# Host-side layout of weights and context in a two-layer gated cross-attention kernel, with values ahead of keys and the first layer's keys made already turned

## The reference

```
x = x + tanh(g_xattn[0]) * attn0(LN(x), ctx, ctx)   # 32 query heads, 8 key/value heads, D = 128,
                                                    # rotary q and k, masked softmax, @ Wo
x = x + tanh(g_ffn[0])   * moe(LN(x))               # 16 experts of 56, top 2, silu(gate) * up, down
x = x + tanh(g_xattn[1]) * attn1(LN(x), ctx)        # same sizes; q and k RMS-normed per head, weights given
x = x + tanh(g_ffn[1])   * lora(LN(x))              # 4 adapters of rank 16, top 2, scaled by 4
```

## Time and profile before

| | |
|---|---|
| time, median of 3 runs | 1358.91 us (1358.12 to 1359.04) |
| profiled execution: span from first to last instruction | 1356.7 us |
| PE busy | 1292.6 us (95%), 6801 matmuls |
| DVE, ACT, POOL busy | 837.7, 501.5, 496.4 us (62%, 37%, 37%) |
| mean granted PE clock | 0.982 of full |
| chain that ended last: PE, POOL, DVE, issue | 74%, 9%, 9%, 6% |
| moved by DMA | 106.97 MB |

### The profile page before, as it was taken

How to read it: one execution, slowest core, us unless ns; L and a number is a source line. 1 busy time by engine, 2 the same in 40 slices (tenths; PEclk the granted TensorE clock), 3 DMA queues, 4 the chain that set the end, 5 groups by cost and what they waited for, 6 DMA issues and landing times.

```text
span 1356.7 us, 18171 instructions
## 1 busy us (share of the span) xinstructions
PE 1292.6 (95%) x6801; PEld 1025.9 (76%) x6801; DVE 837.7 (62%) x1519; ACT 501.5 (37%) x779; POOL 496.4 (37%) x322
## 2 busy tenths in 40 slices
PE   7999999889999999999799999999999999999976
PEld 5888887567777777777688887677777777777765
DVE  4465354888878887888863234655554555555586
ACT  3343242113222222121443124654455455545522
POOL 6302302548677777785301110032332323233200
PEclk9999999889999999999899999999999999999987
DMA  7363555611222222113010004212121121211001
GB/s 263 103 185 128 183 155 179 209 47 63 78 70 70 77 70 69 47 48 109 1 55 32 1 0 118 78 40 71 40 70 70 46 87 53 70 39 39 32 1 62
DMA packets 77500, 106.97 MB, mean 79 GB/s; under 512 B 8108, under 2 KB 40884, under 8 KB 77448
## 3 DMA queue, kind: packets, MB, share of 16 engines
q1 hardware_dynamic: 76808, 104.69, 23.4%
q0 software_dynamic: 640, 1.57, 0.3%
HBM read 78.99 MB, written 27.26 MB: 78 GB/s over the span
## 4 chain that ended last, share of the span: by engine, by line
PE 74%; POOL 9%; DVE 9%; issue 6%; ACT 1%; DMA 1%; SPq 1%; POOLq 0%; DVEq 0%; ACTq 0%
PE ps_q L215 12%; PE ps_q L217 11%; PE ps_q L216 11%; PE ps_b L215 9%; PE ps_b L217 9%; PE ps_b L216 8%; PE ps_s L876 3%; PE ps_s L862 2%; PE ps_b L898 2%; POOL qT L1101 2%; POOL wo_lo L1096 2%; POOL wq_lo L690 1%; PE ps_s L257 1%; PE ps_b L458 1%; POOL p_sb L741 1%
## 5 line engine op out<-in xcount | busy, mean ns | idle before, releaser
L215 PE MATMUL ps_b<-wo_hi,o_hi 128*128 128x512 f32 x512 | 205.8, 402 | 18.2 <-POOL wo_lo L1096 12.3
L215 PE MATMUL ps_q<-hT_hi,wq_hi 128*128 128x512 f32 x512 | 211.4, 413 | 5.4 <-DVE q_t L1176 2.8
L217 PE MATMUL ps_q<-hT_hi,wq_lo 128*128 128x512 f32 x512 | 203.1, 397 | 0.0
L216 PE MATMUL ps_q<-hT_lo,wq_hi 128*128 128x512 f32 x512 | 203.1, 397 | 0.0
L217 PE MATMUL ps_b<-wo_hi,o_lo 128*128 128x512 f32 x512 | 201.4, 393 | 0.0
L216 PE MATMUL ps_b<-wo_lo,o_hi 128*128 128x512 f32 x512 | 200.9, 392 | 0.0
L215 PEld LDWEIGHTS ps_q<-hT_hi,wq_hi 128*128 128x128 f32 x512 | 96.6, 189 | 45.4 <-issue 19.0
L1251 DVE SCALAR_TENSOR_TENSOR x_sb<-ps_b,gates,x_sb 128x512 f32<-128x512 f32 x128 | 92.8, 730 | 58.4 <-PE ps_b L217 57.9
L215 PEld LDWEIGHTS ps_b<-wo_hi,o_hi 128*128 128x128 f32 x512 | 97.4, 190 | 40.8 <-issue 18.1
L1242 DVE TENSOR_TENSOR o_lo<-ps_b,o_hi 128x512 fp32r<-128x512 f32 x128 | 82.1, 683 | 65.0 <-ACT o_hi L1025 64.6
L217 PEld LDWEIGHTS ps_q<-hT_hi,wq_lo 128*128 128x128 f32 x512 | 96.5, 189 | 23.8
(11 more groups left out here) (246 smaller groups left out, 2459.1 us busy)
## 6 DMA issues: line engine op xcount, KB each, us to landing
wq_raw<-in_L_xattn_Wq SPq DMA_DIRECT2D x16, 1024.0 KB, 5.2
wo_raw<-in_L_xattn_Wo SPq DMA_DIRECT2D x16, 1024.0 KB, 5.3
kT_spill<-kT_st SPq DMA_DIRECT2D x4, 2048.0 KB, 6.9
v_hi_spill<-vs_hi SPq DMA_DIRECT2D x16, 512.0 KB, 5.5
v_lo_spill<-vs_lo SPq DMA_DIRECT2D x16, 512.0 KB, 7.2
kT<-kT_spill SPq DMA_DIRECT2D x32, 256.0 KB, 3.4
v_hi<-v_hi_spill SPq DMA_DIRECT2D x16, 512.0 KB, 3.6
v_lo<-v_lo_spill SPq DMA_DIRECT2D x16, 512.0 KB, 4.5
```

The costliest lines, as they stand in the source:

```text
L215: nc.tensor.matmul(dst, l_hi, r_hi, start=first, stop=False)
L216: nc.tensor.matmul(dst, l_hi, r_lo, start=False, stop=False)
L217: return nc.tensor.matmul(dst, l_lo, r_hi, start=False, stop=last)
```

## The change

The host passes every array in the layout in which the core wants it (`laid_out`): the context transposed, every weight transposed where it was (out, in), cut into groups and partition-major, both masks in their final layout, router and adapter weights padded to 128 columns. So PE turns no weight and no context, and each load is one transfer with long rows: the masks are one transfer instead of 16 and 4, gates one instead of two, adapters two instead of six. In particular:

- Start: the first block's work is cut by the contraction: SP loads piece k of the weights and of the context's first half in turn, ACT and DVE split them, and PE adds piece k into four banks for token tiles 0 to 3, then takes tiles 4 to 7. Position ids come through ACT's queue; ACT makes one dummy Sqrt first. One rotation table, eight indirect DMAs.
- Keys and values: the order in a column block is values 0, keys 0, values 1, keys 1, on four banks (`ps_q`, `ps_b[0:2]`); turns of layer-1 keys use `ps_b[2:4]`. Layer-0 keys are computed as (head width x tokens), weights as the stationary side, so they need no turn: DVE rotates with three operations, POOL adds straight into the staging buffer. Weight splits of the next block: ACT and POOL.
- The factor 1/sqrt(D) moves from the query table into the exponential of the first attention.
- Second attention: Wq and Wo are split like those of the first (ACT, POOL); ACT's four Wo splits stand before the first queries of the step.
- Experts: `split_high` on ACT in the old order; low parts of router and gate on DVE, of up and down on POOL.

```diff
+        BLOCKS = (("v", 0), ("k", 0), ("v", 1), ("k", 1))
+        kv_banks = [ps_q[0], ps_q[1], ps_b[0], ps_b[1]]
         def prep_sync(sp):
+            for k in range(KC):
+                sp.dma_start(kw_raw[0][:, k, :], wv0[0, :, k, :]).then_inc(kv[f"first{k}"], 16)
+                sp.dma_start(c_raw[:, k, 0:HALF], ctx_t[0, k]).then_inc(c[f"ctx{k}"], 16)
+            for k in range(KC):
+                sp.dma_start(c_raw[:, k, HALF:T], ctx_t[1, k]).then_inc(c[f"ctx{KC + k}"], 16)
+            kv_sync_load(sp, 1)
...
         def prep_act(act):
+            act.dma_start(pos_i[:, :], pos).then_inc(c["pos"], 16)
+            act.wait_ge(c["consts"], 4)
+            nc.scalar.activation(ln_sd_sb[:, 0:1], zero_b[:, 0:1], ACT.Sqrt, bias=eps_ln[:, 0:1]).then_inc(c["table"], 1)
...
         def kv_sync(sp):
+            for n in range(4 * NB):
+                kv_split_wait(sp, n)
+                if n + 2 < 4 * NB:
+                    kv_sync_load(sp, n + 2)
+                elif n % 2 == 0:
                     att_load_wq(sp, 0, 0)
+                if n == 1:
+                    att_load_mask(sp)
+                kv_sync_spill(sp, n)
+            att_wq_split(sp, 0, 1)
+            att_load_wq(sp, 0, 1)
...
         def kv_pe(pe):
+            for k in range(KC):
+                pe.wait_ge(c["w0_lo"], k + 1)
+                pe.wait_ge(prep["ctx_lo"], k + 1)
+                for i in range(4):
+                    last = three(kv_banks[i][:, :], cT_hi[:, k, i * P:(i + 1) * P], cT_lo[:, k, i * P:(i + 1) * P],
+                                 kw_hi[0][:, k, :], kw_lo[0][:, k, :], k == 0, k == KC - 1)
...
+                    if (kind, lay) == ("k", 0):
+                        g, half = divmod(i, 2)
+                        own, col = slice(half * HALF, (half + 1) * HALF), slice(g * D, (g + 1) * D)
                         for k in range(KC):
+                            last = three(bank[:, :], kw_hi[w][:, k, col], kw_lo[w][:, k, col], cT_hi[:, k, own], cT_lo[:, k, own],
+                                         k == 0, k == KC - 1)
...
+                    if (kind, lay) == ("k", 1) and i >= 1:
+                        keys_t(cb, i - 1)
+                    if b == 0 and n and i == 0:
+                        keys_t(cb - 1, NT - 1)
+            keys_t(NB - 1, NT - 1)
...
         def att_act(act, lay, beside):
             def step(g, h, do_project, do_score, do_finish, next_wq):
                 if do_score and lay:
                     norms(us)
-                if do_finish and h == 0 and lay == 0 and not (isinstance(g, int) and g == 1):
+                if do_finish and h == 0 and not (isinstance(g, int) and g == 1):
                     for j in range(J):
                         wo_high(g - 1, j)
...
-                if lay and do_finish and h == 0:
-                    wo_turn(g - 1)
...
-                    if lay and next_wq:
-                        att_wq_turn(pe, g + 1, t)
...
         def att_pool(pool, lay):
+                if second_first_scores(lay, g, h):
+                    for j in range(J):
+                        wo_low(0, j)
+                        att_wq_low(pool, lay, 1, j)
                     return
...
+                for j in range(J):
+                    wo_low(G - 1, j)
                 att_mask(pool, lay, 2 * G - 1, 1)
...
         def moe_pe(pe):
-            pe.wait_ge(c["w_lo"], 1 + 2 * FT)
+            pe.wait_ge(c["w_lo"], 1 + FT)
+            pe.wait_ge(c["w_lo_pool"], FT)
             up(0, 0, 0)
...
         def moe_pool(pool):
+            for n in range(FT):
+                split_low(pool, 1 + FT + n, "w_lo_pool")
             pool.wait_ge(*att[0]("y_added", 2 * G * PAIRS))
...
             tokens(0, 0)
             tokens(1, 1)
+            for n in range(FT):
+                split_low(pool, 1 + 2 * FT + n, "w_lo_pool")
             tokens(2, 0)
...
+            for j in range(J):
+                att_wq_low(pool, 1, 0, j)
...
         def moe_act(act):
             for m in (20, 21):
-                turn_act(act, m)
+                split_high(act, m)
             tokens(3, 1)
```

More of the change, by code:

```diff
@@ new lines, in prep_act @@
+        def prep_act(act):
+            c = prep
+            act.dma_start(pos_i[:, :], pos).then_inc(c["pos"], 16)
+            act.wait_ge(c["consts"], 4)
+            nc.scalar.activation(ln_sd_sb[:, 0:1], zero_b[:, 0:1], ACT.Sqrt, bias=eps_ln[:, 0:1]).then_inc(c["table"], 1)
+            for m in range(2 * KC):
+                k, half = m % KC, m // KC
+                if half == 0:
+                    act.wait_ge(kv[f"first{k}"], 16)
+                    nc.scalar.activation(kw_hi[0][:, k, :], kw_raw[0][:, k, :], ACT.Copy).then_inc(kv["w_hi"], 1)
+                act.wait_ge(c[f"ctx{m}"], 16)
+                own = slice(half * HALF, (half + 1) * HALF)
+                nc.scalar.activation(cT_hi[:, k, own], c_raw[:, k, own], ACT.Copy).then_inc(c["ctx_hi"], 1)
@@ L354, in prep_act @@
[L354 to L366 removed]
+            pe.wait_ge(c["rope"], 16 * NT)
@@ L493, in kv_weights_hi, with keys_t @@
[L493 to L500 removed]
+            def keys_t(cb, i):
+                pe.wait_ge(c["k_done1"], NT * cb + i + 1)
+                if cb or i >= 2:
+                    pe.wait_ge(c["k_staged1"], NT * cb + max(i - 1, 0))
+                for g in range(GB):
+                    last = nc.tensor.transpose(ps_b[2 + i % 2][:, g * P:(g + 1) * P], k_t1[:, i % 2, g * D:(g + 1) * D], ident[:, :])
+                last.then_inc(c["k_t"], 1)
@@ new lines, in kv_dve @@
+            for n in range(4 * NB):
+                cb, b = divmod(n, 4)
+                kind, lay = BLOCKS[b]
+                if n == 1:
+                    dve.wait_ge(prep["tables"], 4)
+                for i in range(NT):
+                    if kind == "v":
+                        values_lo(n, i)
+                    elif lay == 0:
+                        rotate_key(cb, n, i)
+                    else:
+                        normed_key(cb, n, i)
+                    if n == 2:
+                        ln_stat(dve, lns[0], i, lambda i: (prep["x"], 16))
+                    if n == 3 and i in (2, 5):
@@ L1303, in step @@
                     turn_scores(us, 1 - h)
-                if do_finish and lay and h == 0:
-                    for j in range(J):
-                        wo_low(g - 1, j)
                 rotated(1)
@@ L1420, in turn_bank @@
-        def turn_bank(m):
-            return ps_b[2 + m % 2] if turns[m][0] == "d" else ps_q[m % 2]
-        def turned(m):
-            w, n = turns[m]
-            bank = turn_bank(m)
-            view = bank.rearrange("p (k i) -> p k i", k=KC)
+        splits = [("r", 0)] + [(w, n) for w in "gud" for n in range(FT)]
+        SPLITS = {(0, -1): (0, 1), (0, 0): (2, 3), (0, 1): (4,), (0, 2): (5,), (0, 3): (6, 7),
+                  (1, 0): (8,), (1, 1): (9, 10), (1, 2): (11, 12), (1, 3): (13, 14)}
@@ new lines, in split_parts, with split_high @@
+            return raw[:, :, own], hi[:, :, own], lo[:, :, own]
+        def split_high(act, m):
+            w, n = splits[m]
+            if n == 0:
+                act.wait_ge(moe[f"{w}_in"], 16)
+            if m == 0:
+                act.wait_ge(*att[0]("scored", 2 * G))
+            if (w, n) == ("u", 0):
+                act.wait_ge(*att[0]("o_done", 4 * 2 * G))
+            if (w, n) == ("d", 0):
+                act.wait_ge(*att[0]("y_done", 4 * 2 * G))
+            raw, hi, lo = split_parts(m)
+            nc.scalar.activation(hi, raw, ACT.Copy).then_inc(moe["w_hi"], 1)
```

759 lines of the change are left out of this document (277 added, 482 removed).

## The result

The kernel after takes 1322.25 us (median of four runs, 1320.95 to 1322.49) against 1358.51 for the kernel before on the same chip: ratio 0.973, 95% interval 0.972 to 0.975. It is faster by 36 us; the prediction was 1303, with 1295 to 1320 as its range. The sign was right, the size too large by 19 us. The profiled execution of after has a span of 1320.5 against 1356.7. Later runs were made on other occasions, in which the kernel before itself took 1361 to 1364; so I compare spans of profiled executions, and quote medians beside them. The kernel after was not run again on those occasions. A gain of under 3 us is therefore read from where it arises in the traces, not from the totals.

The account below looks back on a forecast made before the run. PE was taken to bound the key stage and the steady second attention. Gains of 30.6 (start through scores), 2.4 (middle) and 22.6 (second attention) sum to 55.6 us, span 1301.1; plus 2.2, forecast 1303, range 1295 to 1320.

Parts of the forecast that it names:

- Parts 1 to 5: From the start through the first attention's first scores: gains summing to 30.6 us, with +11.1 from the earlier start.
- Part 3: Key and value stage: the remaining 2.6 us are waits on a two-bank ring; four banks and values first give +2.4.
- part 2: Key and value stage: 32 groups of turns removed at 0.48 us each, +15.4 us.
- Part 5: Passage into the first attention: scores no longer wait for kT (1.97) or run at half clock (1.6), +3.6 us.
- Part 6: First attention: steady part unchanged; at its end 13 groups of turns gone at 0.44 us each, net +5.1 us.
- Part 7: Before the first expert tile: new PE wait of 1 to 4 us for POOL's `u` splits and token copy, -3.0 taken.
- Part 8: Expert stage: five groups of `d` turns gone, +2.2 us; new 3.0 wait before the third tile and half clock, -3.8.
- Parts 10 and 11: Second attention: Wo turns off PE's path seven times, +13.3 us; Wq turns gone, +12.9 us.
- Part 12: Second attention: ACT's Wo splits ahead of the first queries make PE wait 0.4 us seven times, -2.8 us.
- B: Rival: half the second attention's gain given back, its Wo gain going into ACT's order; 1318 us, chance 0.18.
- C: Rival: slower than before, through the DVE and POOL port lock in the second attention's units; 1366 us, chance 0.02.
- D: Rival: key stage gains 8 to 12 us less, PE starting its steady work near 15; 1313 us, chance 0.12.

Follow-up runs that it names:

- experiment 7: Kernel after with four extra turns of the identity, unused by the outputs, behind each of the sixteen second-layer value tiles; span 1329.3 us, one execution.
- experiment 1: Kernel after with DVE's six low halves of the gate weights moved from between the last softmax's steps to behind its last residual addition; median 1318.1 us.
- experiment 2: Kernel after with POOL's copy of the third expert tile's tokens ahead of its last two down-weight splits; median 1316.9 us.
- experiment 4: Kernel after with POOL's four low halves of the second attention's first output weights behind the first unit's softmax; median 1322.4 us.
- Experiment 5: Kernel after with, at the second attention's start, last queries before exponentials, POOL's output-weight splits behind the softmax, and second unit's norms before high probabilities; median 1313.2 us.
- experiments 3: Kernel after with ACT's last queries of the second attention's second unit ahead of the first unit's exponentials; median 1321.35 us.

## Why the prediction was right in sign and wrong in size

Of the 19.4 missing, 5.5 lie in the key stage, 6.1 at the end of the first attention, 1.4 in the expert stage, 4.1 at the start of the second attention, 2.3 in its steady part.

Parts 1 to 5, key stage. Right in kind: PE bound, start 10.2 of 11.1, passage to the scores 3.6 of 3.6 (no wait for kT, scores in 1.95). The start was 7.26 instead of 6.4, as ACT copies weights and context in a row (4.74, 5.39) and DVE's first split waited until 5.83 behind the position arithmetic. The first 12 matmuls ran at half clock until 12.1, 2.3 lost where before it was 1.8. Part 4 was too dark: 2.24 instead of 3.4. Part 3 was mis-sized: it read the 2.6 that its budget did not explain as waits. The profile of the kernel before has one wait of 0.86 in this stage besides the 1.46:

```profile
25.79 0.66 PE L458 MATMUL ps_b<-ident,k_t 128*128 128x128 f32 x4 [0.86 <-POOL k_t L578]
```

After has 1.8 in steady blocks (turns of keys and layer norm on DVE, 0.75 the longest), so part 3 is about -1.0, not +2.4. That leaves some 13.6 for part 2 instead of 15.4, by subtraction. Four turns cost 0.44 (experiment 7) instead of 0.48. And there is a loss that no term has: the 2.72 between tiles holds in PE's own rows of the kernel before (208.15 to 221.75, five in a row) and for the first-layer key tiles of after, but the value tiles of after, also without turns, stand 2.80 apart. They are twelve matmuls of the same shapes in the same order as before. In some 25 such tiles that is 2 us; why they take longer no run tells. Part 5's 3.6 is in part luck: at the first values only 2.4 of it is left (276.69 and 252.82), as the softmax chain ends last there in both kernels, and a shorter half-clock stretch behind them (3.4 us instead of 10.2) brings the rest back.

Part 6, end of the first attention: predicted +5.1, and it is -2.5 (PE ready for the first expert tile at 671.3). This is the step that failed worst. It subtracted 13 groups of turns from PE's time, as if PE bound that stretch. DVE's chain into `x_sb` was next in line already in the kernel before, DVE and then PE there:

```profile
670.12 0.75 DVE L1251 SCALAR_TENSOR_TENSOR x_sb<-ps_b,gates,x_sb 128x512 f32<-128x512 f32 x1 [0.62 <-PE ps_b L217]
```
```profile
671.02 0.39 PE L898 MATMUL ps_b<-p_hi,v_hi 64*128 64x256 f32 x2
```

DVE waited 0.62 for PE there, and PE's last values start 0.15 behind the end of `x_sb`. So of the six groups of turns ahead of these values (2.6) little more than 0.6 could be had at all, an estimate from these two rows. Then the chain got longer: the three gate pieces in it take 3.5 more than before. From the last scores to these values PE needs 28.96 instead of 26.49; with the splits out of the chain (experiment 1) it is 24.29. The other seven groups stood behind the values and gave nothing either (22.9 from there to the first expert tile's readiness in both kernels): the longer wait brought a half-clock stretch, 12 matmuls in 5.4 that take 2.8.

Why the chain got longer is the source of an operand. The low part of a gate piece is the same subtraction on the same engine in the same place, and because it now reads SBUF instead of PSUM it waits for POOL. The Trainium skill, "SBUF — State Buffer", section "SBUF: two separate sides", says just this: a VectorE operation with two SBUF inputs contends, against a GpSimd operation that reads SBUF, for the shared pair as an exclusive lock. The trace agrees (2.3 to 2.4 beside POOL, 0.68 and 0.61 without it, and 0.61 to 0.69 beside POOL when one input was in PSUM). I had quoted the lock and missed that condition; I looked for it in POOL's added work, and not in DVE operations whose source changed.

Part 7: the wait is 1.48 (predicted 1 to 4; -3.0 taken), a number that fits better than its working. Counted from the last scores PE was ready at 51.9 instead of the 44.5 of the prediction, and the copy on POOL was there at 53.4 instead of 45.6 to 48.5, as both hang on the same chain; the six splits took 1.26 each, the low end of their price. Part 8: the wait of 3.06 and its half clock, right to a few tenths (experiment 2; -2.0 over both terms against -1.6). Part 9: 0.9 of 1.9; the wait for `hdT_lo` grew from 1.06 to 1.94 as PE came earlier.

Parts 10 and 11, second attention. The first group was to gain 2.4 and lost 1.7: the prediction costed POOL's splits at this start at nothing, while eight of them now stand beside a softmax that DVE makes alone. Four of them moved away bring the second scores 3.0 earlier (experiment 4), but the half clock behind PE's wait takes that back. Experiment 5 gives 8.1, of which experiments 3 and 4 apart give under one. So lock, ACT's order and clock are all in it; how the 4.1 missing here divide among them stays open. In a steady group the 32 turns were worth 3.57 (59.75 less twice 28.09) instead of 3.97; six times 0.4 is the 2.3. Part 12 was right in kind, and in its total by luck: 0.56 in each of five groups, 2.8, for 0.4 in each of seven. Part 13: -0.75 for -0.8, but this stretch alone takes 82.9 to 85.1 in the kernels of the experiments, so the agreement says little.

Of the rivals, B came nearest in time (1318, measured 1322) for the wrong reason: the second attention's steady part kept its gain. C had the right mechanism in the wrong place; it never decided in the steady steps. D named the key stage, where 5.5 were missing, but not its cause: the start was at 7.26, not near 15.

## What to carry to other kernels

When an operand moves from PSUM to SBUF, the instruction that reads it can change its price even if nothing else does: look at which DVE operations then have two SBUF inputs, and what POOL does in that moment. Removed PE work is only worth something where PE ends last in that very stretch; at a seam, follow the chain that ends last and count what is queued on it. Count both kernels' repeated unit over many repetitions in the bound engine's own rows: a tile of twelve matmuls that is 2.72 in one kernel can be 2.80 in the next, and a remainder in a budget is not a wait until the profile shows one. And add up single gains only after a look at whether two of them remove the same stretch.

## What was not expected of the hardware

DVE operations differ in what POOL does to them. Beside POOL's splits, tensor-tensor operations on SBUF and small copies were held up (0.19 to 1.16, 0.73 to 1.88 or 4.00 for four), while 32x32 block transposes and reductions kept their 1.25 and 1.22. And the same idle of 1.94 before the same 21 matmuls (`hdT_lo`) was free in ten of the kernels here and cost 1.6 in three others through the granted clock. The tail, the same work in all thirteen, takes 82.9 to 85.1 us, with 23.8 to 31.4 us of it at the lower level. What decides it was not tried.
